# Statistics of a unit one pair earlier: the order of VectorE, ScalarE and GpSimd in pass 0 of a cross attention

## Reference

```
xn = layernorm(ctx)                          # 4096 x 256
ln = layernorm(layernorm(x))                 # 256 x 256
q  = ln @ Wq                                 # 16 heads of 64
k, v = concat([xn @ Wkv, ln @ Wkv])          # 4352 keys
qn = rmsnorm(q) * scale ; kn = rmsnorm(k)
out = softmax(qn @ kn.T) @ v                 # per head
x  = x + out @ Wout + bout
```

## Time and profile before

| | us |
|---|---|
| median of 3 runs (lowest, highest) | 673.33 (672.17, 673.88) |
| time of the profiled execution | 672.22 |
| its span | 670.5 |
| busy: TensorE matmul, weight load | 651.6 (97%), 522.4 (78%) |
| busy: VectorE, ScalarE, GpSimd | 511.7 (76%), 414.2 (62%), 271.8 (41%) |

### The profile page before, as it was taken

How to read it: one execution, slowest core, us unless ns; L and a number is a source line. 1 busy time by engine, 2 the same in 40 slices (tenths; PEclk the granted TensorE clock), 3 DMA queues, 4 the chain that set the end, 5 groups by cost and what they waited for, 6 DMA issues and landing times. The chain is left out here.

```text
span 670.5 us, 14507 instructions
## 1 busy us (share of the span) xinstructions
PE 651.6 (97%) x5192; PEld 522.4 (78%) x5192; DVE 511.7 (76%) x1008; ACT 414.2 (62%) x880; POOL 271.8 (41%) x211
## 2 busy tenths in 40 slices
PE   8899999999999999999999999999999999899998
PEld 7677777777777777777777777777775778899998
DVE  4888898877878777778767867877777685987674
ACT  5788788866566666665667566556563433655651
POOL 3544545533443443433443434434431300364640
PEclk9999999999999999999999999999999999999999
DMA  7111340010000010000000000000000301566500
GB/s 213 56 44 33 112 162 1 17 33 1 1 17 1 2 49 1 1 1 1 17 1 1 2 0 2 1 17 2 1 1 1 127 1 65 189 212 218 163 33 17
DMA packets 26164, 30.51 MB, mean 46 GB/s; under 512 B 4201, under 2 KB 23794, under 8 KB 26098
## 3 DMA queue, kind: packets, MB, share of 16 engines
q1 hardware_dynamic: 24594, 28.86, 13.1%
q10 hardware_dynamic: 1504, 0.79, 0.4%
HBM read 29.38 MB, written 0.26 MB: 44 GB/s over the span
## 5 line engine op out<-in xcount | busy, mean ns | idle before, releaser
L897 POOL TENSOR_TENSOR k_rms<-k_ss,neg_half 128x4 f32<-128x4 f32 x136 | 189.2, 1391 | 242.7 <-DVE k_ss L771 242.7
L603 ACT ACTIVATE probs<-s_ps,minus_bound 128x512 f32<-128x512 f32 x272 | 164.7, 689 | 97.0 <-PE s_ps L436 97.0
L169 PE MATMUL kv_ps<-w_quad,xn 128*128 128x512 f32 x816 | 206.9, 402 | 5.2 <-DVE xn L718 3.9
L765 DVE SCALAR_TENSOR_TENSOR probs_sum<-probs,tile_mask,probs_sum 128x512 f32<-128x512 f32 x264 | 191.8, 744 | 4.9 <-ACT probs L603 4.8
L169 PEld LDWEIGHTS kv_ps<-w_quad,xn 128*128 128x128 f32 x816 | 147.8, 188 | 44.5 <-DVE xn L718 6.6
L449 PE MATMUL o_ps<-probs,v 128*64 128x256 f32 x1088 | 132.6, 385 | 0.8 <-ACT probs L603 0.7
L436 PEld LDWEIGHTS s_ps<-q_parts,kt 64*128 64x128 f32 x1632 | 101.2, 185 | 26.6 <-issue 20.0
L436 PE MATMUL s_ps<-q_parts,kt 64*128 64x256 f32 x1632 | 115.0, 287 | 0.3 <-DVE kt L775 0.2
L449 PEld LDWEIGHTS o_ps<-probs,v 128*64 128x64 f32 x1088 | 71.9, 136 | 42.0 <-issue 10.9
L749 DVE SCALAR_TENSOR_TENSOR kn<-k_rms,kv_ps 128x256 f32<-128x256 f32 x136 | 56.8, 417 | 53.0 <-POOL k_rms L897 51.8
L771 DVE TENSOR_REDUCE k_ss<-k_sq 128x4 f32<-128x256 f32 x136 | 56.4, 415 | 21.0 <-ACT k_sq L581 20.0
(11 more groups left out here) (212 smaller groups left out, 647.3 us busy)
## 6 DMA issues: line engine op xcount, KB each, us to landing
w_raw<-in_ffn_W SPq DMA_DIRECT2D x18, 1024.0 KB, 5.6
rows<-in_ctx SPq DMA_DIRECT2D x7, 512.0 KB, 4.0
w_raw<-in_L_xattn_Wkv SPq DMA_DIRECT2D x6, 256.0 KB, 3.4
wout<-in_L_xattn_Wout SPq DMA_DIRECT2D x4, 256.0 KB, 2.8
wq_raw<-in_L_xattn_Wq SPq DMA_DIRECT2D x3, 256.0 KB, 2.8
rows<-in_ctx SPq DMA_DIRECT2D x2, 256.0 KB, 5.3
w_raw<-in_L_xattn_Wkv ACTq DMA_DIRECT2D x2, 256.0 KB, 5.2
wq_raw<-in_L_xattn_Wq ACTq DMA_DIRECT2D x1, 256.0 KB, 4.3
```

What stands on the lines that cost most here:

```text
L169: last = nc.tensor.matmul(out, stationary(k, s), moving(k, m), start=n == 0, stop=n == len(terms) - 1)
L603: nc.scalar.activation(probs[n % P_RING][:, :, c, :], s_ps[n % 2][c][:], ACT.Exp, bias=minus_bound[:]).then_inc(exp_done, 1)
L765: nc.vector.scalar_tensor_tensor(total, probs[n % P_RING][:, :, c, :], seen, total, ALU.mult, ALU.add).then_inc(sum_done, 1)
L897: nc.gpsimd.tensor_tensor(k_rms[n % 2][:].rearrange("p i c -> p (i c)"), k_ss[n % 2][:].rearrange("p i c -> p (i c)"), neg_half[:, 0:4], A ...
```

## The change

No instruction is added or taken away. In pass 0:

- VectorE's `statistics` go from behind the first addition of a pair to the end of the pair before it, behind the last `kn` (and for unit 4 into the start). GpSimd's `root_of` goes with them, from ahead of the two `root` to behind them.
- On VectorE `offset` and `center` now stand ahead of the first `mean_square` of the pair, and in the start `rest(2)` and `mean_square(3)` stand ahead of `offset(3)` and `center(3)`.
- ScalarE's `center(3)` in the start goes between the exponentials of step 0 and those of step 1.
- The two low parts of pass 1's weights, which stood together at the end of pair 15, go between the first two additions of that pair and ahead of its last `kn`.

```diff
--- before.py
+++ after.py
@@ -634,13 +634,14 @@
             gain(2)
             square(3)
             keep_v(3)
-            center(3)
             act.wait_ge(bound_done, 1)
             for m in range(STEPS // 2 + 1):
                 e = 2 * m
                 for n in (e - 2, e - 1):
                     if exists(n):
                         weights(n)
+                    if n == 0:
+                        center(3)
                 for t in range(1, NPASS):
                     if m == query_pair(t, 3):
                         keep_qt(t)
@@ -828,25 +829,26 @@
             kt_rest(1)
             statistics(3)
             scale_k(2)
+            rest(2)
+            mean_square(3)
             offset(3)
             center(3)
-            rest(2)
-            mean_square(3)
             scale_k(3)
+            statistics(4)
             dve.wait_ge(mask_done, 1)
             for m in range(STEPS // 2 + 1):
                 e = 2 * m
                 if exists(e - 2):
                     add_weights(e - 2, 0)
-                if m and m + 1 in unit_of:
-                    statistics(unit_of[m + 1])
+                if m == weights_pair(1) + 1:
+                    weights_lo(1, 0)
                 if exists(e - 2):
                     add_weights(e - 2, 1)
-                if m and exists(e + 2):
-                    mean_square(e + 2)
                 if m and m + 1 in unit_of:
                     offset(unit_of[m + 1])
                     center(unit_of[m + 1])
+                if m and exists(e + 2):
+                    mean_square(e + 2)
                 if exists(e - 2):
                     add_weights(e - 1, 0)
                 for n in (e, e + 1):
@@ -859,8 +861,12 @@
                     add_weights(e - 1, 1)
                 if m and m in unit_of:
                     rest(unit_of[m])
+                if m == weights_pair(1) + 1:
+                    weights_lo(1, 1)
                 if m and exists(e + 2):
                     scale_k(e + 3)
+                if m and m + 2 in unit_of:
+                    statistics(unit_of[m + 2])
                 for t in range(1, NPASS):
                     if m == query_pair(t, -1):
                         queries_lo(t)
@@ -871,7 +877,7 @@
                     if m == query_pair(t, 3):
                         qt_rest(t)
                     for k in range(KD):
-                        if m == (NU - 2 if t == 1 else weights_pair(t) + 1 + k):
+                        if t > 1 and m == weights_pair(t) + 1 + k:
                             weights_lo(t, k)
                 if m == NU + 1:
                     dve.wait_ge(bout_in, 16)
@@ -936,16 +942,17 @@
             root(2)
             root_of(3)
             root(3)
+            root_of(4)
             nc.gpsimd.memset(fw.proj_bd[:], 0.0).then_inc(fw.blocks_zeroed, 1)
             nc.gpsimd.memset(fw.diag_bd[:], 0.5 * DHP ** -0.5).then_inc(fw.blocks_started, 1)
             nc.gpsimd.memset(fw.pair_mask[:], 1.0).then_inc(fw.blocks_started, 1)
             for m in range(STEPS // 2):
                 e = 2 * m
-                if m and m + 1 in unit_of:
-                    root_of(unit_of[m + 1])
                 if m and exists(e + 2):
                     root(e + 2)
                     root(e + 3)
+                if m and m + 2 in unit_of:
+                    root_of(unit_of[m + 2])
                 for t in range(1, NPASS):
                     if m == query_pair(t, 0):
                         root_q(t)
```

## The result

The changed kernel takes 674.25 us (median of 16 runs, 673.08 to 675.27) beside 673.37 of the kernel before (16 runs on the same chip); the ratio is 1.0020, 95% interval 1.0012 to 1.0028, that is 0.8 to 1.9 us slower. By the bound of 0.3% this is no change; the ratio says 1.3 us slower, the two medians 0.9, and 1.2 was forecast.

A forecast was written before the change was run, and what follows sets the result against it. TensorE is busy 97%, but the VectorE loop through GpSimd makes a pair 7.64 us. 2.3 us later at pair 13 less 1.1 for the low parts gives 1.2 slower: median 674.5, range 670.0 to 676.5.

The forecast's parts named there:

- The fact that decides: A VectorE addition holds a GpSimd operation starting under it until 0.60 after the addition's start; a reduction does not.
- part (a): VectorE and GpSimd in a pass 0 pair: rstd and both k_rms held, loop 7.97 instead of 7.64, 0.33 longer.
- Rival 1: rstd isn't held by the second addition: loop 7.59, 3.1 us faster, 670.2; chance 12%.
- Rival 2: Nothing gets in between two additions, so var_eps is held until 2.55: loop 8.26, 4.6 us slower, 677.9; chance 8%.
- Part (b): The start: kn of step 3 at 25.83, a lead of 1.01; second kn of pair 1 at 33.27.
- Part (c): Sum at pair 13: ten loops of 7.97 put TensorE's projection at 120.7 instead of 118.39, 2.3 later.
- part (e): The rest: ScalarE's center in the start, SyncE's row loads and GpSimd's selects of pair 10 cost nothing.
- Part (d): Low parts of pass 1's weights: TensorE's wait of 1.06 goes whole, minus 1.1 with the step between matmuls.
- Rival 3: The low parts save nothing because a late kn takes their place: 2.3 slower, 675.6; chance 5%.
- Sum: Whole kernel: 2.3 - 1.1 = 1.2 us slower; predicted median 674.5, or 0.2% more.
- rival 4: The main case, 1.2 slower, with 0.2 of rounding per ten loops and 0.5 for the start: 673.3 to 675.7; 66%.

The follow-up runs named there:

- experiment 1: Changed kernel with its second addition in pairs 2 to 13 replaced by a reduction: pass 0 loop 7.59 instead of 7.95; 669.43 us, one run, only its trace used.
- experiment 2: Changed kernel with each kt_rest put directly behind a mean_square: loop 7.62, 0.33 shorter; 671.45 us, one run, only its trace used.
- experiment 3: Changed kernel with the first mean_square of a pair between the two additions: 666.49 us, ratio 0.9907 to the kernel before.
- experiment 5: Kernel before with the start of the change alone, without statistics(4) in the start: 671.69 us, ratio 0.9988.
- the second kernel of 6: Changed kernel with mean_square between the two additions and GpSimd's four selects moved from pair 10 to 30: 666.03 us, ratio 0.9917 to the kernel before.

## Why the prediction was right

*The fact that decides, and part (a).* That an addition holds GpSimd's operation, and that two additions back to back would put `rstd` under one, was the step on which the sign hung. Each number of it came out within 0.05: `rstd` 1.07 (1.05 to 1.1 forecast), both `k_rms` 1.44 and 1.45, `mean_off` at 3.27 (3.30), loop 7.95 (7.97), idle of TensorE 0.55 (0.55). VectorE's waits for `k_rms` were 0.23 and 0.30 where I said 0.27 and 0.35: the profile counts them from the end of the instruction ahead, I from the step, which ends a little sooner. Experiments 1 and 2 show the cause by taking it away at one place and then at the others: 0.36 per loop for `rstd` (7.95 to 7.59), and 0.33 for both `k_rms`. One comparison is not as even as it looks: the loop that ends at the projection of pair 13 takes 7.92 in the kernel before already (110.47 to 118.39; VectorE's first addition waits 0.19 there for ScalarE, which has just made a part of the query weights) and 7.96 in the changed one. So the change costs 0.31 in an ordinary loop and 0.04 in that one.

Rival 1 would have needed an `rstd` of 0.72 under an addition; in the changed kernel none is. Rival 2 is out as well: `var_eps` starts under the first of two additions in a row and ends at 67.24, 0.79 after that addition's start and not behind the second.

*Part (b), the start.* `kn` at 25.87 (25.83 forecast), `mean_off` at 28.60 (28.60), second `kn` of pair 1 at 33.36 (33.27). Alone it is worth 0.8. That these positions agree so well is in part luck. This execution ran 0.13 earlier than the one that the forecast was read from (the statistics of unit 3 start at 22.01 instead of 22.14), and the `k_rms` that was priced at 1.01 takes 1.18, by the timelines of VectorE and GpSimd:

```profile
24.56 0.41 DVE L713 TENSOR_SCALAR z<-rows,mean_var,rstd 128x256 f32<-128x256 f32 x1
...
24.65 1.18 POOL L903 TENSOR_TENSOR k_rms<-k_ss,neg_half 128x4 f32<-128x4 f32 x1 [0.52 <-DVE k_ss L772]
```

It starts 0.09 into a `center`, a `tensor_scalar` with a single input from SBUF, and all runs that have the new start show this 1.17 to 1.18. The prediction let the short additions of pair 1 hold GpSimd and left out this hold of 0.17.

*Part (c).* T13 at 120.77 (120.7). Less the 0.13 by which this execution ran early, it is 0.2 late, which part (e) accounts for.

*Part (d), the low parts.* 1.15 (1.1), without a new wait; 1.1 alone by the times. Rival 3 falls: the `k_rms` ahead of the second low part, 142.08, takes 1.44 like the others, and `kn` waits 0.30.

*Part (e), where I said "nothing", is the step that failed:* the selects of pair 10 cost 0.18. I had put them into a gap of GpSimd by their lengths of before, and the rule of the hold, which I had just worked out, holds selects too. GpSimd's timeline in pair 10 of the changed kernel:

```profile
107.08 1.07 POOL L922 TENSOR_TENSOR rstd<-var_eps,neg_half 128x2 f32<-128x2 f32 x1
...
108.97 0.76 POOL L965 TENSOR_SCALAR_AFFINE_SELECT f_pair_mask<-f_pair_mask 88x34 f32<-88x34 f32 x1
109.71 1.00 POOL L903 TENSOR_TENSOR k_rms<-k_ss,neg_half 128x4 f32<-128x4 f32 x1
```

The last select takes 0.76. The same one takes 0.53 in the kernel before, where it starts under an addition too, and 0.22 in experiment 3, where it doesn't. `k_rms` behind it ends at 110.71, where it would end at 110.52 by the distance of the other pairs. In T13 the selects' 0.18 and the 0.17 of the start don't show: the other nine loops are 0.02 shorter each than I priced them, and the execution began 0.13 earlier.

*Sum:* 1.23 later at T16, 1.24 at the last projection of pass 3 (500.79 beside 499.55), 1.2 forecast; 1.3 by the ratio. The parts add up: 3.3 for the loop (T13 - T2 is 87.65 instead of 84.37), less 0.9 for the start (T2), less 1.15 for the low parts, gives 1.25. With the 0.13 by which the execution began earlier, the change costs 1.4, a little more than forecast. The times say so too, by the two groups into which the last section divides them by the clock: their medians are 673.44 before and 674.91 changed in the one, 671.94 and 673.54 in the other, that is 1.5 and 1.6 later. The ratio over all runs says less, because the groups are not of the same size in both kernels. So the mechanism and the sign were right, and that the sum met 1.2 so closely owes a few tenths to terms that cancel.

One line of the prediction doesn't come out of its own terms: 0.2 of rounding and 0.5 for the start around 674.5 give 673.8 to 675.2, not 673.3 to 675.7 (rival 4). The width beyond that is a guess.

## What to carry to other kernels

When a short GpSimd operation lies on a loop through VectorE, look at what VectorE runs in the moment at which it starts, not only at how long it has to finish. Moving a wait earlier can put it under an instruction with two SBUF inputs, and the hold (0.35 to 0.44 for each inverse root here) eats the gain; a reduction or an instruction with one operand from PSUM in that place cost nothing here. Here one line of order more, the reduction between the two additions, turned 0.2% slower into 0.9% faster.

And when a loop is only 4% above TensorE's own pace, price the whole way around it, through each engine, before and after; the number of instructions ahead of one wait says little.

## What the runs showed of the hardware

*The hold.* A GpSimd `tensor_tensor` or `tensor_scalar` that starts while VectorE runs an instruction with two SBUF inputs of 128x512 gets going about 0.60 after that instruction's start (`k_rms` 1.45 instead of 1.01, `rstd` 1.07 instead of 0.71). The select under such an addition gets going 0.60 after its start as well (0.76 instead of 0.22). Under a reduction of nearly the same length (0.68) and under `kt_rest`, with one operand from PSUM, nothing is held: in experiment 2 a `k_rms` that starts 0.16 into a `kt_rest` takes 1.01, in pair 10 of the changed kernel one that starts 0.14 into it takes 1.00. It isn't the width of 512 either: in the start of the changed kernel a `k_rms` starts at 17.48, 0.08 into `qn` (128x512 at 17.40 for 0.69, one operand from PSUM), and takes 1.01. One form with a single SBUF input does hold, `tensor_scalar`: under the first additions of pair 1 (two of 128x512 in 0.85) `rstd` takes 0.81, and under a `center` of 128x256 (0.41) `k_rms` takes 1.18. The Trainium skill (SBUF — State Buffer, section Who interferes with whom) names these cases, the last one as a fast mode that uses both ports. It also says that the order of issue decides who blocks, and of that fast mode that whoever comes first has the shared pair for the whole instruction. For two SBUF inputs the rows don't bear out that a GpSimd instruction which comes first blocks VectorE: in the earlier trace rows an addition starts at 68.66, in the middle of a `k_rms` from 68.20 to 69.21, and takes its usual 0.75.

*The clock.* Not expected: in the profiled execution of the changed kernel TensorE's granted clock falls in the experts, after TensorE had been idle 1.87 before 581.06.

```profile
580.00:582.00 2.00, 0.94 (x8) 0.94 (x9) 2.00 (x3) 0.90 (x3) 1.05 (x1) 1.00 0.05 18
582.00:584.00 2.00, 2.00 (x14) 2.00 (x13) 2.00 (x2) 0.67 (x2) 0.00 (x0) 0.61 0.03 8
584.00:586.00 2.00, 2.00 (x9) 1.71 (x9) 1.83 (x3) 0.48 (x1) 0.00 (x0) 0.53 0.54 132
586.00:588.00 2.00, 2.00 (x15) 1.64 (x14) 1.97 (x3) 2.00 (x2) 0.00 (x0) 1.00 1.14 373
```

A row has the stretch, its length, the busy times (and counts) of TensorE, its weight load, VectorE, ScalarE and GpSimd, and then the granted clock (the last two columns are the share of the DMA engines and GB/s): 0.61 and 0.53, so mostly the lower of the two levels, 1.2 instead of 2.4 GHz, for some 3 us. The distance from the projection after that idle to the next one is 5.59 (581.06 to 586.65), where it is 4.08 before (579.82 to 583.90), with an idle of 1.89 ahead and no fall. That is 1.5 us. Of the 16 runs of the changed kernel, the 8 with a mean clock of 0.997 lie at 674.66 to 675.27, the 8 with 1.000 at 673.08 to 673.85. The times of the kernel before fall into two such groups as well (5 at 671.6 to 672.2, 11 at 673.2 to 673.9; in the sets beside the experiments its runs from 673.35 up have a mean clock of 0.997 and those up to 672.95 one of 0.999 or 1.000), so the change is not what brings it about. The other traces say the same: TensorE's idle at that place is 1.88 to 1.89 in the five with a mean clock of 1.000 (before, experiments 1, 3 and 5, and the second kernel of 6), without a fall, and 1.87 to 2.28 in the five below 1.000, each with a fall behind it. So the length of the idle alone doesn't tell them apart. What decides it in a given execution is open; nothing was tried on it.
